# The causal mask of the maximum pass: one product over 64 rows in place of two

## What is computed

```python
x = x + 0.5 * ffn(layernorm(x), ...)      # two experts of eight per sample
x = x + attn(layernorm(x), Wqkv, Wo)
x = x + 0.5 * ffn(layernorm(x), ...)

def attn(x, Wqkv, Wo):                    # 16 heads of 16 features
    qkv = x @ Wqkv.T                      # q and k are then rotated by position (rope)
    scores = einsum('bhqd,bhkd->bhqk', q, k) / sqrt(16)
    scores = where(causal, scores, -inf)  # key <= query
    return softmax(scores) @ v @ Wo.T
```

## Time and profile before

| | |
|---|---|
| median of 3 runs | 2402.93 us (2398.98 to 2409.86) |
| the profiled execution | 2401.97 us |
| its span, first to last instruction | 2400.2 us |
| attention, PE's first to last product | about 445 to 1996 us of the span |
| busy share of the span, PE / DVE / ACT / POOL | 91% / 82% / 57% / 53% |
| mean granted clock of TensorE | 0.979 of full speed |

### The profile page before, as it was taken

One profiled execution on the slowest core, in us unless ns is written; L12 is line 12 of the kernel. 1 busy time (PEld: TensorE's weight loads), 2 busy tenths in 40 slices (PEclk: granted clock), 3 DMA queues, 4 the chain that ended last, 5 costly groups with the idle time before them and its releaser, 6 DMA issues. The chain is left out here.

```text
span 2400.2 us, 56572 instructions
## 1 busy us (share of the span) xinstructions
PE 2190.0 (91%) x19596; PEld 1279.8 (53%) x19596; DVE 1956.3 (82%) x4345; ACT 1357.7 (57%) x2567; POOL 1280.2 (53%) x1458
## 2 busy tenths in 40 slices
PE   2999999399999999999999999999999986999999
PEld 1666666245554555555455455545545543666666
DVE  4777777379989989998998999899899864777776
ACT  2455545046666666666666666666666663455454
POOL 3666666335545544554554555455455424666664
PEclk9999999779999999999999999999999997999999
DMA  5566665323444444344344434444433513665664
GB/s 162 172 203 204 203 204 191 88 63 89 97 89 93 95 92 90 89 99 89 93 95 89 90 90 99 89 96 94 86 90 92 93 39 111 187 210 193 208 205 164
DMA packets 280284, 295.50 MB, mean 123 GB/s; under 512 B 45664, under 2 KB 263104, under 8 KB 280000
## 3 DMA queue, kind: packets, MB, share of 16 engines
q1 hardware_dynamic: 279456, 290.83, 46.8%
q10 hardware_dynamic: 544, 1.05, 0.1%
HBM read 140.08 MB, written 83.89 MB: 93 GB/s over the span
## 5 line engine op out<-in xcount | busy, mean ns | idle before, releaser
L817 ACT ACTIVATE at_probs<-at_st_ps 128x512 f32<-128x512 f32 x1280 | 748.2, 604 | 508.6 <-PE at_st_ps L924 499.1
L750 DVE TENSOR_REDUCE at_mx<-at_mx_ps 128x1 f32<-128x512 f32 (+3 forms) x1408 | 839.8, 634 | 141.3 <-PE at_mx_ps L905 139.6
L672 POOL TENSOR_SCALAR_AFFINE_SELECT at_probs<-at_probs 128x512 f32<-128x512 f32 x512 | 320.5, 639 | 710.6 <-ACT at_probs L817 710.6
L899 PE MATMUL at_mx_ps<-at_k_stack,at_q_stack 48*128 48x512 f16 (+3 forms) x2048 | 502.3, 303 | 20.7 <-DVE at_mx L750 10.7
L924 PE MATMUL at_st_ps<-at_q_stack,at_k_stack 49*128 49x512 f16 (+3 forms) x2048 | 459.5, 302 | 65.7 <-ACT at_probs L817 64.2
L428 ACT ACTIVATE f_h<-f_h_ps,f_b1s 128x512 f32<-128x512 f32 x256 | 176.0, 688 | 359.2 <-PE f_h_ps L470 347.7
L924 PEld LDWEIGHTS at_st_ps<-at_q_stack,at_k_stack 49*128 49x128 f16 x2048 | 135.8, 94 | 433.4 <-ACT at_probs L817 332.0
L904 PE MATMUL at_mx_ps<-mask,turn 64*128 64x128 bf16 (+2 forms) x1408 | 342.2, 243 | 0.0
L941 PE MATMUL at_pv_ps<-at_probs,at_v 128*32 128x512 f32 (+3 forms) x4096 | 331.4, 441 | 0.3 <-POOL at_probs L672 0.3
L905 PE MATMUL at_mx_ps<-mask,turn 64*128 64x64 bf16 (+2 forms) x1408 | 281.5, 200 | 0.0
L486 PE MATMUL f_y_ps<-f_w2hi,f_hlo 128*128 128x256 f16 x1024 | 279.1, 273 | 0.0
(11 more groups left out here) (118 smaller groups left out, 4240.0 us busy)
## 6 DMA issues: line engine op xcount, KB each, us to landing
at_q_stack<-qk_image SPq DMA_DIRECT2D x192, 128.0 KB, 4.3
at_k_stack<-qk_image SPq DMA_DIRECT2D x192, 128.0 KB, 4.4
f_x<-in_x SPq DMA_DIRECT2D x32, 512.0 KB, 5.6
f_w1hi<-w_hi SPq DMA_DIRECT2D x128, 128.0 KB, 2.3
f_w1lo<-w_lo SPq DMA_DIRECT2D x128, 128.0 KB, 2.1
f_b2s<-in_b SPq DMA_DIRECT2D x128, 128.0 KB, 3.7
f_w2hi<-w_hi SPq DMA_DIRECT2D x128, 128.0 KB, 4.2
f_w2lo<-w_lo SPq DMA_DIRECT2D x128, 128.0 KB, 4.2
```

Source lines behind the costliest of these rows:

```text
L672: nc.gpsimd.affine_select(out=ap, in_=ap, compare_op=ALU.is_ge, fill=0.0, base=0, pattern=[[0, d] for d in dims] + [[1, P]], channel_multi ...
L750: nc.vector.tensor_reduce(o_ap, i_ap, AX_X, ALU.max).then_inc(max_done, 1)
L817: nc.scalar.activation(probs[:, c, :], st_ps[c % 2][:], ACT.Exp, scale=DH ** -0.5).then_inc(exp_done, 1)
L899: nc.tensor.matmul(bank[:, at * w:at * w + w], q_stack[s.par][rows, j + a, i * P:(i + 1) * P], k_stack[s.par][rows, j + a, 0:w], start=(at ...
```

## The change

The mask becomes one product over 64 rows. Row r of the tables stands for the pair of keys 2r and 2r+1. `turn` holds for a query q in row r: 2^64 if q < 2r, 2^-20 if q = 2r, and 0 otherwise. `mask` holds for key 2r the value -2^-24, for key 2r+1 the value -2^60, and 0 elsewhere. So the product gives at least 2^40 in size, negative, wherever the key lies ahead of the query, 0 where it doesn't, and -2^-44 on the even diagonal. L904 keeps its shape and now carries the semaphore; L905 is gone. `turn` shrinks from 192 to 128 columns. The tables are built with four `affine_select` over 64 x 128 in place of three smaller ones, and SP copies both tables to the upper partitions, which is one DMA more.

```diff
@@ build_tables, SP
-            sp.wait_ge(half_masked, 1)
+            sp.wait_ge(half_masked, 2)
+            sp.dma_start(tab.turn[HP:P, :], tab.turn[0:HP, :]).then_inc(loaded["b1"], 16)
             sp.dma_start(tab.mask[HP:P, :], tab.mask[0:HP, :]).then_inc(loaded["b1"], 16)
-            sp.wait_ge(loaded["b1"], 32)
+            sp.wait_ge(loaded["b1"], 48)
@@ build_tables, DVE
-            dve.wait_ge(tables_done, 8)
+            dve.wait_ge(tables_done, 7)
@@ build_tables, POOL
-            nc.gpsimd.memset(tab.mask[:], -1e30).then_inc(ident_zeroed, 1)
+            nc.gpsimd.memset(tab.mask[:], 0.0).then_inc(ident_zeroed, 1)
...
-            nc.gpsimd.affine_select(out=tab.turn[:, HP:P], in_=tab.turn[:, HP:P], compare_op=ALU.not_equal, fill=1.0,
-                                    base=0, pattern=[[-1, HP]], channel_multiplier=1).then_inc(ident_zeroed, 1)
-            pool.wait_ge(ident_zeroed, 4)
-            nc.gpsimd.affine_select(out=tab.turn[:, HP:P], in_=tab.turn[:, HP:P], compare_op=ALU.not_equal, fill=1.0,
-                                    base=-HP, pattern=[[-1, HP]], channel_multiplier=1).then_inc(tables_done, 1)
-
-            nc.gpsimd.affine_select(out=tab.mask[0:HP, 0:HP], in_=tab.mask[0:HP, 0:HP], compare_op=ALU.is_gt, fill=0.0,
-                                    base=0, pattern=[[1, HP]], channel_multiplier=-1).then_inc(half_masked, 1)
+            q_of, k_of = tab.turn[0:HP, :], tab.mask[0:HP, :]
+            nc.gpsimd.affine_select(out=q_of, in_=q_of, compare_op=ALU.is_ge, fill=2.0 ** 64,
+                                    base=0, pattern=[[1, P]], channel_multiplier=-2).then_inc(ident_zeroed, 1)
+            nc.gpsimd.affine_select(out=k_of, in_=k_of, compare_op=ALU.not_equal, fill=-2.0 ** -24,
+                                    base=0, pattern=[[1, P]], channel_multiplier=-2).then_inc(ident_zeroed, 1)
+            pool.wait_ge(ident_zeroed, 5)
+            nc.gpsimd.affine_select(out=q_of, in_=q_of, compare_op=ALU.not_equal, fill=2.0 ** -20,
+                                    base=0, pattern=[[1, P]], channel_multiplier=-2).then_inc(half_masked, 1)
+            nc.gpsimd.affine_select(out=k_of, in_=k_of, compare_op=ALU.not_equal, fill=-2.0 ** 60,
+                                    base=-1, pattern=[[1, P]], channel_multiplier=-2).then_inc(half_masked, 1)
@@ attention_phase, PE, max_scores
-                nc.tensor.matmul(last, tab.turn[const, HP:3 * HP], over.broadcast_to([HP, nh, P]), start=False, stop=False)
-                nc.tensor.matmul(last[:, :, HP:P], tab.turn[const, 0:P], over[:, :, 0:HP].broadcast_to([HP, nh, HP]),
-                                 start=False, stop=True).then_inc(mx_done, 1)
+                nc.tensor.matmul(last, tab.turn[const, :], over.broadcast_to([HP, nh, P]), start=False, stop=True).then_inc(mx_done, 1)
@@ program
-        tab.turn = sb("turn", [P, 3 * HP], BF16)
+        tab.turn = sb("turn", [P, P], BF16)
```

## The result

The changed kernel takes 2370.21 us (median of 4 runs, 2368.52 to 2377.44), the kernel before 2404.89 us beside it. The medians are 35 us apart. The ratio is 0.9863, with a 95% interval of 0.9831 to 0.9894: 33 us less, by the interval 25 to 41. I had forecast 2375 us and a range of 2352 to 2392. The profiled execution took 2371.06 us, 30.9 us less than the 2401.97 us of the one before.

A forecast was written before the change was run, and what follows sets the result against it. DVE (21.8 us) and PE (24.8 us) were taken to bound each sample in turn. L905's 1.03 us in PE's piece less 0.17 leaves 0.86, 27.5 us for 32 samples, off 2401.97: forecast 2375 us, range 2352 to 2392.

The forecast's parts named there:

- The time: Whole kernel: 2375 us, with a sample of 45.7 us in place of 46.58.
- Two pieces that hand over to each other: In each sample DVE sets the pace from (0,5) to (2,5), 21.8 us, and PE from there to (0,5), 24.8 us.
- The price of L905 by columns: Each L905 costs PE 0.033 us with 64 columns, 0.06 with 128, 0.115 with 256: 0.43 ns a column, 0.005 us a product.
- The gain in PE's piece: Units (2,5) through g = 3 to (0,5), 23 in all: 1.03 us a sample, 0.86 after the waits for ACT.
- No gain in DVE's piece: From (0,5) to (2,5) nothing is gained: PE would come earlier and wait longer, at (1,10) and (2,5).
- my rivals with the two lengths: DVE meets POOL at more places; one more L731 at 1.25 us, not 0.68, costs 18 us: 2393 us, chance 0.12.
- The wait for ACT swallows what lies in units 6 and 7: PE waits at unit 8 for unit 6's exponential; savings at (2,6), (2,7), (3,5), (3,6), (3,7) vanish, 0.17 us a sample.
- PE all the way: Rival: DVE's piece is shorter than it looks, so all four slots gain, 1.7 us a sample, 54 us: 2348 us, chance 0.15.
- The clock: Rival: PE's longer waits in DVE's piece lower its clock; one sample in 32 costs 25 us, two give 2425; chance 0.03.
- The tables: At the kernel's start, one more SP copy and three or four small POOL operations, hidden by 18 us of cover.
- What the profile after would show: L905 gone, L904 unchanged, DVE's waits for L904 around 85 us from 112, PE's for DVE 20 to 30 from 10.

## Why the prediction came out right, and where it was off

- *The time.* 2375 forecast, 2370.2 measured; a sample 45.7 forecast, 45.57 measured.
- *Two pieces that hand over to each other.* Right, and shown: the product costs 27 us when it stands in one piece and 10 in the other, and each time the other piece stays the same within 0.03 us.
- *The price of L905 by columns.* Right in kind, a little too high in size. The times between the ends of the products that release DVE, unit by unit before and after, shrink by 0.028 to 0.030 us at most of the units with 64 columns, by 0.056 with 128 and by 0.108 with 256; I had 0.033, 0.06 and 0.115. That makes 0.93 us for the 23 units in place of 1.03. The run with 8 columns leaves about 0.003 us for a product beside its columns, where I took 0.005.
- *The gain in PE's piece.* 0.86 us a sample forecast, 0.70 measured (24.29 to 23.59). The steps that were mis-sized are the price, by which 0.10 is missing, and the list of waits that swallow something. I had only the waits for ACT in it, with 0.17 us. The wait for DVE's low half L778 before the transposes at (3,4) was not in my list: the time from the product of (3,4) to that of (3,5) grew from 1.40 to 1.47 us where it should have shrunk by 0.03, and so it took 0.10. All other waits together took what remains by subtraction, 0.93 - 0.10 - 0.70 = 0.13 us and not 0.17.
- *No gain in DVE's piece.* Wrong in size: it gained 0.31 us (22.29 to 21.98). The step "in DVE's piece nothing is gained" took the durations of DVE's rows as given. L731 is 0.06 us shorter at (1,0) and 0.22 at (1,3), which makes 0.28. The mechanism stood among my rivals with the two lengths, but I had it as a chance of a loss, or of the whole gain. I didn't ask which way a faster PE moves the mask against L731. The two errors, 0.16 too much and 0.31 too little, partly cancel. That the time came out within 5 us is luck to that extent.
- *The wait for ACT swallows what lies in units 6 and 7.* Right: 384 more columns there cost nothing.
- *PE all the way.* It did not come, and the pair of runs with less work for DVE shows that even then it would have been 39 us and not 54. The rival was priced as if L731 would no longer meet POOL, and in those runs it stands behind POOL for longer than before.
- *The clock.* It did not fall inside attention here, once the lower stretches at its beginning are over (at 534 us). The run with the late statistics shows that the risk was real: with PE's waits of 0.96 and 0.38 us at (2,7) and (2,8) it fell in 11 of 27 samples. But I had the price wrong. I took 25 us for one sample at the lower level, and a fall took 1.5 to 3.3 us there.
- *The tables.* As forecast, no cost: the last copy is issued at 13.50 us, DVE's last table starts at 31.30.

```profile
13.50 0.58 SPq L138 DMA_DIRECT2D mask<-mask  x1
```

```profile
31.30 0.68 DVE L162 TENSOR_TENSOR wo_lo<-wo_stage,wo_hi 128x512 f16<-128x512 f32 x1
```

- *What the profile after would show.* DVE's waits for the mask's product are 102.9 us and not the 85 of the forecast, since DVE's own work became shorter too. PE's waits for DVE, 17.6 us, are a little under the 20 to 30.

## What to carry to other kernels

Where two engines are both nine tenths busy, look for the places where the one's wait ends and the other's begins, and count a saving only in the stretch in which its engine sets the pace; putting the removed work back in one stretch at a time shows it cleanly. Price the removed product by the distance between starts, never by the duration of its row. And ask of each DVE row in the path that reads two operands from SBUF whether a POOL row is running when it starts: that is time that a shift of any third engine can give or take. A wait that is filled with the next piece of work helps only where that work's own input is ready.

## What the hardware showed that I had not expected

L731, with both operands in SBUF, does not run slower beside a POOL instruction, it stops until that one ends. Its length is 0.55 us and the rest of POOL's row at its start, and at least 0.67: 0.49 left gives 1.04, 0.28 gives 0.82, 0.37 gives 0.92, and with 0.14 us of lead for DVE it takes 0.68 and POOL's row becomes 0.39 us longer. The sum holds in all 14 kernels of this case, for 63 to 94 rows of L731 in each that start with more than 0.13 us of POOL's rope or mask to go: the constant is 0.54 or 0.55 us in all of them. Rows that read one operand from PSUM, such as L724, keep their 0.68 us beside POOL, here in the kernel before:

```profile
1002.66 0.68 DVE L724 TENSOR_TENSOR at_by_cos<-at_x_ps,at_cos 128x512 f32<-128x512 f32 x1
```

```profile
1001.98 1.27 POOL L682 TENSOR_TENSOR at_rotated<-at_by_cos,at_by_sin 128x512 f32<-128x512 f32 x1
```

The Trainium skill (SBUF — State Buffer, section "Who interferes with whom") describes a port pair that DVE and GpSimd share as an exclusive lock: whoever issues first holds it, and a DVE instruction with two SBUF inputs contends with a GpSimd instruction that reads SBUF. These rows agree with it, in both orders.

One row of POOL is an exception. L731 at (2,3) starts while POOL takes a power of 128x4 elements and takes its 0.68 us all the same (1022.88 in the earlier trace rows), with 0.89 us of this row to go:

```profile
1022.75 1.02 POOL L696 TENSOR_TENSOR at_rstd<-at_ve,minus_half 128x4 f32<-128x4 f32 x1
```

So it is in some 29 samples of the kernel before. That row reads SBUF too, but very little; why it doesn't stop DVE no run here shows.

The other thing is the clock. In the changed kernel it is 1.00 from 540 to 1900 us, with a wait of up to 0.6 us in nearly every slot and one of 1.3 us. With the late statistics PE waits 0.96 and 0.38 us more in each sample, and behind that the granted clock fell to 1.2 GHz in 11 of 27 samples and stayed in the others.
